# First expert stage of a four-layer graph network: logits and mixing weights turned in blocks of two tiles, and three VectorE operations reordered

## The reference

```
gp = softmax(xf @ Wr + br)                    # 4 groups
ep = softmax(einsum('nd,gde->nge', xf, Wgate) + bgate)   # 4 experts in each group
# of each softmax the best two are kept, the second only while the running sum is <= 0.9,
# and renormalised: w_group [N,4], w_exp [N,4,4]
tw = (w_group[:, :, None] * w_exp * 0.5).reshape(N, 16)
for e in range(16):
    h = silu(xf @ W1[e]) * (xf @ W3[e])       # 32 hidden units an expert
    out = out + tw[:, e:e+1] * (h @ W2[e])
x = x + out
```

## Time and profile before

| | |
|---|---|
| time, median of 3 runs | 2504.57 us (2501.77 to 2507.76) |
| profiled execution: span, first to last instruction | 2499.5 us |
| stage of the change in it | from about 404 to about 1240 us |
| granted TensorE clock, whole span | 0.971 |
| TensorE busy | 94% |
| VectorE / ScalarE / GpSimd busy | 71% / 45% / 28% |

### The profile page before, as it was taken

One profiled execution on the slowest core, in us unless ns is written; L12 is line 12 of the kernel. 1 busy time (PEld: TensorE's weight loads), 2 busy tenths in 40 slices (PEclk: granted clock), 3 DMA queues, 4 the chain that ended last, 5 costly groups with the idle time before them and its releaser, 6 DMA issues. The chain is left out here.

```text
span 2499.5 us, 33408 instructions
## 1 busy us (share of the span) xinstructions
PE 2347.8 (94%) x10818; PEld 1857.9 (74%) x10818; DVE 1766.1 (71%) x4177; ACT 1135.5 (45%) x2077; POOL 688.4 (28%) x627
## 2 busy tenths in 40 slices
PE   6899895999999999999789999999997899999998
PEld 4677674777777777778667888888875677777776
DVE  7588796787777878786565765555565677777775
ACT  6564323444445453535342222222235666566641
POOL 6465013212222212110122222121233333333310
PEclk9899997999999999999899999999998999999999
DMA  5121133212121212121263343433357566666631
GB/s 167 52 53 51 18 135 107 82 54 101 52 101 55 97 56 97 55 93 45 95 208 108 130 143 127 137 129 130 130 167 201 123 148 145 160 160 148 147 97 47
DMA packets 155873, 271.89 MB, mean 109 GB/s; under 512 B 35538, under 2 KB 36178, under 8 KB 155478
## 3 DMA queue, kind: packets, MB, share of 16 engines
q1 hardware_dynamic: 123014, 203.00, 24.6%
q0 software_dynamic: 32720, 67.19, 11.7%
HBM read 185.82 MB, written 100.41 MB: 115 GB/s over the span
## 5 line engine op out<-in xcount | busy, mean ns | idle before, releaser
L2389 ACT ACTIVATE conv_h<-conv_h 128x512 f32<-128x512 f32 x79 | 50.0, 633 | 305.4 <-DVE conv_h L2318 279.7
L2870 POOL DMA_INDIRECT next_own<-message,net_slot_d x75 | 123.2, 1642 | 163.1 <-DMA next_own<-own 145.8
L2287 DVE TENSOR_TENSOR conv_yl<-conv_pty,conv_yh 128x512 fp32r<-128x512 f32 x79 | 54.7, 692 | 148.4 <-ACT conv_yh L2379 139.6
L1024 POOL DMA_INDIRECT early_val<-values,net_slot_s x79 | 85.3, 1080 | 189.8 <-DVE d_x L1502 88.6
L68 PE MATMUL d_po<-shared_wq_hi,d_hh 128*128 128x512 f32 x316 | 130.7, 414 | 7.3 <-DVE d_hl L1508 3.3
L1733 ACT ACTIVATE d_act_out<-d_pa 128x512 f32<-128x512 f32 (+1 forms) x80 | 46.2, 577 | 197.6 <-PE d_pa L70 197.6
L68 PE MATMUL conv_p<-conv_w_hi,conv_yh 128*128 128x512 f32 x316 | 132.3, 419 | 1.6 <-DVE conv_yl L2287 1.6
L68 PE MATMUL d_pc<-d_xh,shared_wv_hi 128*128 128x512 f32 (+1 forms) x320 | 129.3, 404 | 0.0
L68 PE MATMUL d_pa<-d_xh,xp_w_hi 128*128 128x512 f32 (+1 forms) x320 | 128.7, 402 | 0.0
L69 PE MATMUL conv_p<-conv_w_lo,conv_yh 128*128 128x512 f32 x316 | 126.0, 399 | 0.0
L70 PE MATMUL conv_p<-conv_w_hi,conv_yl 128*128 128x512 f32 x316 | 125.9, 398 | 0.0
(11 more groups left out here) (622 smaller groups left out, 7201.9 us busy)
## 6 DMA issues: line engine op xcount, KB each, us to landing
conv_yin<-y SPq DMA_DIRECT2D x79, 256.0 KB, 2.8
h<-conv_h SPq DMA_DIRECT2D x79, 256.0 KB, 2.0
own<-xp_own_buf SPq DMA_DIRECT2D x79, 256.0 KB, 2.0
next_own<-own SPq DMA_DIRECT2D x79, 256.0 KB, 4.4
next_x<-y SPq DMA_DIRECT2D x79, 256.0 KB, 3.0
out<-d_res SPq DMA_DIRECT2D x79, 256.0 KB, 2.5
y<-d_y SPq DMA_DIRECT2D x78, 256.0 KB
d_x<-in_x SPq DMA_DIRECT2D x10, 1024.0 KB
```

Of the source, the lines that this page charges most:

```text
L1024: pool.indirect_dma_start(early.val[:, t, :], None, k.values[:, :], bass.IndirectOffsetOnAxis(ap=k.slot["s"][:, T * g + t:T * g + t + 1], ...
L2287: v.tensor_tensor(lo[:, t % 2, :], bank[t % 2][:], hi[:, t % 2, :].bitcast(F32), ALU.subtract)\
L2389: act_.activation(h[:, t, :], h[:, t, :], ACT.Relu).then_inc(h_made, 1)
L2870: pool.indirect_dma_start(own[n][:, t, :], None, k.message2[:, :], bass.IndirectOffsetOnAxis(ap=k.slot["d"][:, T * g + t:T * g + t + 1], a ...
```

## The change

- Each of the two halves of 64 rows of the logits' bank now holds the 40 logit rows (the router's weights are written a second time at column 64, L1434 and following in `constants`). ScalarE copies, in two instructions of 64 partitions by 256 columns in place of one of 40 by 512, tiles 0 and 2 to the upper and tiles 1 and 3 to the lower half of `logit_t`, now 128x256.
- TensorE turns that in two transposes of 128x128 against the identity. The sum over the two parts of the weights, done by `fold` before, is a second addition on VectorE, so that routing has 26 steps.
- `parts` has 64 columns a tile, two tiles side by side are one transpose, two in place of four. ScalarE writes the result to `mix_t` in two instructions of 64 partitions by 256 columns; the other half of the rows of `mix_t` is zero from the start, and `expert_r` is written a second time at row 64 (one more VectorE copy of 32x512 before the loop).
- On VectorE the last gate stands ahead of the statistics of g+2; the first of the two BN_STATS follows it, the second is in the routing after step 15. `back(g, 0)` is issued while ScalarE takes the exponential, and `back(g, 1)` after step 11, which is the place where it was.

```diff
 D = 512
+HALF_P = P // 2
...
         wr = early.wr
-        fold = c.sb("fold", [2 * SETS * 4, SETS * 4])
...
         xh, xl = ([c.sb(f"{n}{i}", [P, KC, GR], F32R) for i in range(2)] for n in ("xh", "xl"))
-        logit_t = c.sb("logit_t", [2 * SETS * 4, GR])
+        logit_t = c.sb("logit_t", [P, 2 * P])
...
         mix = c.sb("mix", [P, T, EXPERTS0])
-        parts = c.sb("parts", [P, T, P], F32R)
+        parts = c.sb("parts", [P, T, HALF_P], F32R)
...
         block = stack.enter_context(nc.Block(no_gpsimd_drain=True))
-        NSTAT, NROUTE = 4, 25
+        NSTAT, NROUTE = 4, 26
+        SET4 = SETS * 4
+        pair_rows = [slice(0, HALF_P), slice(HALF_P, P)]
...
             return not isinstance(i, int) or 0 <= c_ + ahead < NG
+
+        def tile_pairs(rows, b):
+
+            return rows[:].rearrange("p (a b n) -> p a b n", a=2, b=2)[:, :, b, :]
...
             def constants():
-                v.memset(wr[:, :, 2 * SETS * 4:P].bitcast(F32), 0.0).then_inc(router_made, 1)
-                v.tensor_tensor(fold[:], k.ident[0:2 * SETS * 4, 0:SETS * 4],
-                                k.ident[0:2 * SETS * 4, SETS * 4:2 * SETS * 4], ALU.add).then_inc(router_made, 1)
-                v.memset(parts[:, :, 2 * EXPERTS0:P].bitcast(F32), 0.0).then_inc(router_made, 1)
+                for b in range(2):
+                    v.memset(wr[:, :, b * HALF_P + 2 * SET4:(b + 1) * HALF_P].bitcast(F32), 0.0).then_inc(router_made, 1)
+                    v.memset(tile_pairs(mix_t, 1 - b)[pair_rows[b]].bitcast(F32), 0.0).then_inc(router_made, 1)
+                v.tensor_copy(wr[:, :, HALF_P:HALF_P + 2 * SET4], wr[:, :, 0:2 * SET4].bitcast(F32)).then_inc(router_made, 1)
+                v.memset(parts[:, :, 2 * EXPERTS0:HALF_P].bitcast(F32), 0.0).then_inc(router_made, 1)
...
-            def front1_begin(i, c_):
+            def front1_begin(i, c_, t):
                 g = i * XS + c_
-                v.wait_ge(x1_made, 4 * g + tiles(g) + 4)
-                if in_range(i, c_, -1):
-                    v.wait_ge(x1_normed, 4 * g)
-                hold(v)
-                for t in range(2):
-                    v.bn_stats(st[1][:, t, :], x[c_ % XS][:, t, :])
+                if t == 0:
+                    v.wait_ge(x1_made, 4 * g + tiles(g) + 4)
+                    if in_range(i, c_, -1):
+                        v.wait_ge(x1_normed, 4 * g)
+                    hold(v)
+                v.bn_stats(st[1][:, t, :], x[c_ % XS][:, t, :])
...
-            def routing(g, between):
+            def routing(g, during_exp, between):
...
                 v.wait_ge(logits_turned, g + 1)
-                link(v.tensor_tensor(prob[:].rearrange("p (t s) e -> p t (s e)", t=T),
-                                     ptr[:, 0:T * SETS * 4].rearrange("p (t n) -> p t n", t=T),
-                                     rbias[:].unsqueeze(1).broadcast_to([P, T, SETS * 4]), ALU.add))
+                flat = prob[:].rearrange("p (t s) e -> p t (s e)", t=T)
+                turned_ = ptr[:, 0:T * HALF_P].rearrange("p (t n) -> p t n", t=T)
+                link(v.tensor_tensor(flat, turned_[:, :, 0:SET4], rbias[:].unsqueeze(1).broadcast_to([P, T, SET4]), ALU.add))
+                link(v.tensor_tensor(flat, turned_[:, :, SET4:2 * SET4], flat, ALU.add))
...
                 s(v.tensor_tensor(prob[:], prob[:], total[:].unsqueeze(2).broadcast_to([P, NS, 4]), ALU.subtract))
+                if during_exp:
+                    during_exp()
...
                         add(g + 2, u2, t)
-                    front1_begin(i, c_ + 2)
                 scale_gate(g, 3)
+                if front:
+                    front1_begin(i, c_ + 2, 0)
...
                 if mid:
-                    routing(g + 1, {6: lambda: back(g, u, 0), 10: lambda: back(g, u, 1)})
+                    between = {11: lambda: back(g, u, 1)}
+                    if front:
+                        between[15] = lambda: front1_begin(i, c_ + 2, 1)
+                    routing(g + 1, lambda: back(g, u, 0), between)
...
             v.tensor_tensor(expert_r[:], expert[:], expert2[:], ALU.add).then_inc(expert_made, 1)
-            front1_begin(0, 1)
+            v.wait_ge(expert_made, 1)
+            v.tensor_copy(expert_r[HALF_P:HALF_P + 2 * EXPERTS0], expert_r[0:2 * EXPERTS0].bitcast(F32)).then_inc(expert_made, 1)
+            front1_begin(0, 1, 0)
+            front1_begin(0, 1, 1)
             v.wait_ge(routed_in, 16)
-            routing(0, {})
+            routing(0, None, {})
...
                 act_.wait_ge(logits_done, g + 1)
-                act_.activation(logit_t[:], ptr[0:2 * SETS * 4, :], ACT.Copy).then_inc(logits_out, 1)
+                for b in range(2):
+                    act_.activation(logit_t[pair_rows[b]].rearrange("p (a n) -> p a n", a=2), tile_pairs(ptr, b)[pair_rows[b]],
+                                    ACT.Copy).then_inc(logits_out, 1)
...
             def softmax_exp(g):
-                act_.wait_ge(route, NROUTE * g + 3)
+                act_.wait_ge(route, NROUTE * g + 4)
...
                 act_.wait_ge(mix_turned, g + 2)
-                act_.activation(mix_t[:], ptr[:], ACT.Copy).then_inc(mix_out, 1)
+                for b in range(2):
+                    act_.activation(tile_pairs(mix_t, b)[pair_rows[b]], ptr[pair_rows[b], 0:2 * P].rearrange("p (a n) -> p a n", a=2),
+                                    ACT.Copy).then_inc(mix_out, 1)
...
             pe.sem_inc(mix_turned, 1)
-            pe.wait_ge(router_made, 3)
+            pe.wait_ge(router_made, 6)
...
                 elif not first:
-                    pe.wait_ge(mix_out, g)
+                    pe.wait_ge(mix_out, 2 * g)
...
             def turn_logits(g):
-                pe.wait_ge(logits_out, g + 1)
-                for t in range(T):
-                    last = pe.matmul(ptr[:, t * SETS * 4:(t + 1) * SETS * 4], logit_t[:, t * P:t * P + P],
-                                     fold[:], start=True, stop=True)
+                pe.wait_ge(logits_out, 2 * g + 2)
+                for a_ in range(2):
+                    last = pe.transpose(ptr[:, a_ * P:a_ * P + P], logit_t[:, a_ * P:a_ * P + P], k.ident[:])
...
                 pe.wait_ge(route, NROUTE * g + NROUTE)
-                for t in range(T):
-                    last = pe.transpose(ptr[:, t * P:t * P + P], parts[:, t, :].bitcast(F32), k.ident[:])
+                for a_ in range(2):
+                    last = pe.transpose(ptr[:, a_ * P:a_ * P + P],
+                                        parts[:, 2 * a_:2 * a_ + 2, :].rearrange("p t n -> p (t n)").bitcast(F32), k.ident[:])
...
                     turn_mix(0)
-                    pe.wait_ge(expert_made, 1)
-                    pe.wait_ge(mix_out, 1)
+                    pe.wait_ge(expert_made, 2)
+                    pe.wait_ge(mix_out, 2)
...
                     up(g, n, 0, "w3", pc, gate_done)
-                    pe.wait_ge(mix_out, g + 1)
+                    pe.wait_ge(mix_out, 2 * g + 2)
...
```

## The result

| | before | after |
|---|---|---|
| median of 4 runs, us | 2504.76 (2501.77 to 2507.76) | 2487.45 (2485.52 to 2494.18) |
| span of the profiled execution, us | 2499.5 | 2492.5 |
| stage, first turned tile to last product of `down`, us | 813.8 | 797.0 |
| steady distance of two turnings of the logits, us | 40.84 | 39.88 |

After over before is 0.9933, with a 95% interval of 0.9917 to 0.9950: 17.3 us less. The forecast was 2486.6 us.

The account below looks back on a forecast made before the run. TensorE was taken as the bound, with the VectorE and ScalarE loop just behind; the loop falling from 40.62 to 39.83 us would set the pace, 1.01 us a group over 18 groups, about 18 us, to 2486.6 us (range 2477 to 2498).

Parts of the forecast that it names:

- second bound: Loop of VectorE and ScalarE round a group needs 40.62 of 40.84 us, so shortening TensorE's work alone gains almost nothing.
- gate first, less the statistic in the routing: VectorE: last gate directly behind the four additions gains 1.38 us a group; one statistic inside the routing costs 0.60.
- second addition: VectorE's routing: the added sum of the logits costs the loop 0.27 us a group, bounds 0.2 and 0.69.
- early `back(g, 0)`: VectorE, during ScalarE's exponential: gains 0.38 us less a 0.10 wait for tile 0's last product, 0.28 a group.
- first to second `back`: VectorE's routing: distance from back(g, 0) to back(g, 1) grows from 2.59 to 3.45 us, giving TensorE a new wait.
- The wait at the 16th product: TensorE in `down`: 0.36 us lost a group waiting for VectorE's last low part; the change was to remove it.
- 0.1 to 0.3 at the later transposes: TensorE's waits at later transposes, us a group, part of what raises its need from 38.77 to about 39.5.
- TensorE's own need of 38.77: TensorE's work a group without waits: 39.89 us less 0.94 (turning the logits) and 0.18 (mixing weights).
- rival 1: TensorE keeps the pace, the loop being looser than read: up to 2.07 us a group, 37 us, 2467; chance 0.08.
- The loop keeping most: Addition at its upper bound and longest back(g, 0) wait leave 0.49 us a group; 7 us, 2497; chance 0.11.
- no change: Pace kept by something neither part touches (norm, transposes, reciprocal root on GpSimd): 2504 us; chance 0.06.
- slower: VectorE's routing becomes the longer arm if the gate's move brings nothing: 8 us more, 2512; chance 0.05.

Follow-up runs that it names:

- e_turn_only: Changed kernel with VectorE's old order put back, keeping block turning and second addition; 2501.17 us, 0.9997 of the kernel before.
- e_gate_late: Changed kernel with both statistics ahead of the last gate again and none in the routing; 2498.16 us, 0.9976 of the kernel before.
- c_all: Changed kernel with front1_end ahead of back_mean, statistics moved into VectorE's two gaps, back(g, 1) one step sooner; 2467.87 us, 0.9853 of the kernel before.
- r_after: The changed kernel run again without an edit; 2482.22 us, 0.9921 of the kernel before.
- e_turn_thrice: Changed kernel with each transpose of the logits issued three times, same output; 2487.40 us, 0.9947 of the kernel before.
- e_swap: Changed kernel with front1_end (the norm's shift) ahead of back_mean on VectorE; 2479.52 us, 0.9910 of the kernel before.
- e_gap: Changed kernel with statistics of g+2 moved into VectorE's waits for ScalarE's high parts; 2474.57 us, 0.9882 of the kernel before.
- e_order_only: Kernel before, turning in eight pieces, with VectorE's whole new order; 2500.07 us, 0.9994 of the kernel before.

## Why the prediction was right

**The bound.** Right. Less work on TensorE alone changed nothing (e_turn_only, group 40.86), as the second bound demanded; the loop without its gate move is at 40.64 (e_gate_late), where the prediction's terms give 40.62 + 0.27 - 0.28 = 40.61.

**The loop's length.** Predicted 39.83; undisturbed groups take 39.80 to 39.83, with the few at 40.1 to 40.2 the mean is 39.88. Term by term:
- gate first, less the statistic in the routing: 0.78, measured 0.84 (e_gate_late). The gate stands 2.41 behind the additions' start; predicted 2.44.
- second addition: 0.27, measured 863.53 to 863.80 = 0.27, and at least 0.27 by the two kernels with a late `back`.
- early `back(g, 0)`: 0.28, measured 0.26 to 0.33. It starts 1.75 behind the low part, predicted 1.82. It does not wait; the same move with the old turning waits 1.32 us.
- first to second `back`: 3.45, measured 864.67 to 868.11 = 3.44.

**TensorE.** The logits' turning was put at 0.26 and is 859.60 to 859.97 = 0.37, less the slot of `spread` 0.23, plus about 0.09 of slow start: 0.23. Gain 0.97 for 0.94. The wait at the 16th product was to go; a rest of it, 0.08 by the slots of before and 0.18 by its own, stays. That at the 25th is gone, and the 37th has the predicted new one: 0.20 to 0.27 late, and 0.11 of slow start on top, against 0.2 to 0.3.

Two terms were off, in opposite directions. "0.1 to 0.3 at the later transposes" was too small: in brackets it is (4.6 + 4.3) / 16 = 0.56 us a group, from start to start 1.03 to 1.09. And TensorE's own need of 38.77 was too high: take all that comes late out of the 39.83, 1.05 at the transposes, 0.18 and 0.27 in `down` and twice the slow start of 0.11, and about 38.1 is left; c_all gives the same (38.90 - 0.8). The difference of 0.7 is the shorter slot of the matmuls, which no term had. Neither did harm, since TensorE was not to set the pace. Had it done so, as in rival 1, up to 40.84 - 38.1 = 2.7 us a group would have come out in place of that rival's 2.07.

The Trainium skill (TensorE: Matmul & The Clock Gate, Part 4: PE-mode transpose) puts a transpose within a kernel at about 275 ns. As a price from start to start it would ask, by an estimate from that page, for 0.55 us for the pair and 1.65 for the six. The traces have 0.13 and 0.57, for fp32, so it does not hold as a price of transposes in a row.

**ScalarE.** The copy of two times 256 columns takes 0.77 us (predicted 0.80, had 0.58 for one of 512), and nothing waits for it. ScalarE's timeline of the changed kernel:

```profile
858.38 0.77 ACT L1761 ACTIVATE d_logit_t<-d_ptr 64x256 f32<-64x256 f32 x2
875.18 0.77 ACT L1771 ACTIVATE d_mix_t<-d_ptr 64x256 fp32r<-64x256 f32 x2
```

**The sum.** 18 distances were to give 18.2 us; they gave 17.4 (between the first `up` products of the second and the last group, 464.92 to 1196.89 before and 472.94 to 1187.55 after). The start was to cost 1 us and cost 0.8. The last two distances among them fell by 0.66 and 1.49 (39.83 to 39.17, 38.59 to 37.10), as much as two steady ones; behind them, where the end was to give about 1 back, only 0.2 came. The stage is 16.8 us shorter, the median 17.3. The stage thus gave 1.2 us less than the sum's 18, and the median fell by 17.3 in the first runs and by 19.7 in r_after. That the first of them lies within 1 us of the forecast is partly luck.

**What the prediction did not see.** It treated the two halves of the change as if their terms could be added. The early `back(g, 0)` is worth 0.28 us only behind a short turning; behind the old one it takes back nearly all the gate gives. And without it the old turning reaches 39.86 in its trace, since TensorE's own need of before, 39.89, lies where the new loop does; by its median it gains 11.7 us and not 17 to 20, and that difference is open. The number was right for the pair; the share of each part was not worked out.

**Rivals.** TensorE keeping the pace falls with the traces of e_turn_only (1.7 us of work gone, the group as before) and e_turn_thrice (0.15 of 0.44). e_swap and e_gap shorten the group without touching TensorE's work; they also take waits from TensorE, so they fit and decide less. The loop keeping most, no change and slower fall with the time itself. The rival on the slower side needed a gate that brings nothing and a statistic in the routing as well. e_gate_late has the first without the second and gives 40.64, still under 40.84; both together were not run.

## What to carry to other kernels

When an engine is busy for 99% of a stretch, still follow the other engines once round the period without it: a second bound within 1%, as here (40.62 of 40.84 us), makes nearly every saving on the first worth nothing until it moves, and e_turn_only (nothing) beside the whole change (17 us) is what that looks like. Read how full TensorE is from start to start, and not from its busy share: a TensorE that is 99.7% busy still took 0.8 us more a group than its work needs (e_order_only). In a queue that runs in order, pull forward what the slowest reader needs and put work that nobody waits for into the gaps where the engine already stands (the gate, e_gap); but before pulling forward an operation that reads another engine's result, work out when that result is there, since a wait there holds all that is queued behind it. When two parts of a change act on two bounds, work out each part alone and both together: the terms do not add.

## What was unexpected of the hardware

- Transposes of 128x128 in a row cost less from start to start than the records' length suggests: two 0.13 us, four 0.36, six 0.57, where the records show 0.38, and 0.81 for the six. Eight small products of 40x20 took 1.00.
- The distance of two 128x512 matmuls in the same stretch of code was 0.234 us in the three kernels with the eight small products and 0.228 to 0.230 in all with transposes of whole blocks, at a granted clock of 1.00 in both; outside the stage it was 0.233 in both. The small products are one of several things that differ; which of them does it was not tried.
- TensorE's granted clock was 1.00 in the steady windows before and after, although it is idle for 13.4 us of 725 (725.00 - 711.57) where it was 7.3; in the attention stage, on unchanged code, it was 0.95 and 0.97 in two executions of one kernel.
